# A conditioned transformer block on one core: attention values in the SwiGLU's two PSUM banks, and new instruction orders on four engines

## The reference

```
g, b = t @ gw.T + gb, t @ bw.T + bb                       # per sequence
rmsnorm(x) = g * x * rsqrt(mean(x*x) + 1e-6) + b
x1  = x + attention(rmsnorm_1(x))                         # 16 heads of 16, softmax(q k^T / 4) v, Wo
y   = x1 + (silu(xn @ gate.T) * (xn @ hid.T)) @ out.T     # xn = rmsnorm_2(x1), hidden size 1024
out = x + y
```

## Time and profile before

| what | value |
|---|---|
| median of 3 runs | 1031.92 us (1028.68 to 1034.21) |
| the profiled execution's own time | 1032.31 us |
| its span in the profile | 1030.2 us |
| PE busy | 962.1 us, 93% of the span |
| DVE, ACT, POOL busy | 68%, 54%, 44% |
| one iteration of the loop (start of `scores(t, 0)` to the next) | 60.3 us |
| first `scores(1, 0)` starts at | 87.95 us |
| last iteration with attention (t = 15) starts at | 934.5 us |

### The profile page before, as it was taken

One profiled execution on the slowest core, in us unless ns is written; L12 is line 12 of the kernel. 1 busy time (PEld: TensorE's weight loads), 2 busy tenths in 40 slices (PEclk: granted clock), 3 DMA queues, 4 the chain that ended last, 5 costly groups with the idle time before them and its releaser, 6 DMA issues.

```text
span 1030.2 us, 24455 instructions
## 1 busy us (share of the span) xinstructions
PE 962.1 (93%) x9136; PEld 818.9 (79%) x9136; DVE 699.1 (68%) x1178; ACT 559.6 (54%) x1271; POOL 452.9 (44%) x393
## 2 busy tenths in 40 slices
PE   5667999999999999999999999999999999999898
PEld 4556887878888787888878788887878788788777
DVE  3465767676776768677676867767687776768652
ACT  4444655555565555646555554655656565565442
POOL 3523534454453445435244543534355353435342
PEclk9888999999999999999999999999999999999999
DMA  4100001010100101000010100001010000100000
GB/s 157 62 2 21 1 3 42 1 41 0 32 9 0 41 0 41 0 24 17 0 41 0 41 0 20 20 0 41 0 41 0 20 20 0 41 0 21 1 21 21
DMA packets 18971, 21.71 MB, mean 21 GB/s; under 512 B 640, under 2 KB 18240, under 8 KB 18816
## 3 DMA queue, kind: packets, MB, share of 16 engines
q1 hardware_dynamic: 18720, 21.24, 6.2%
q10 hardware_dynamic: 224, 0.10, 0.1%
HBM read 12.95 MB, written 8.39 MB: 21 GB/s over the span
## 4 chain that ended last, share of the span: by engine, by line
PE 61%; DVE 15%; ACT 11%; issue 9%; POOL 1%; ACTq 1%; DMA 0%; DVEq 0%; SPq 0%; POOLq 0%
PE ps L830 6%; PE ps L832 5%; PE ps L831 5%; PE ps L942 5%; PE ps L958 5%; PE ps L961 4%; PE ps L959 4%; PE ps L950 4%; PE ps L943 4%; PE ps L907 4%; PE ps L915 4%; PE ps L931 3%; DVE row_max L628 3%; DVE sums L642 3%; ACT xn L361 3%
## 5 line engine op out<-in xcount | busy, mean ns | idle before, releaser
L251 POOL TENSOR_TENSOR h_lo<-h,h_hi 128x512 fp32r<-128x512 f32 x128 | 167.6, 1309 | 98.9 <-ACT h_hi L411 92.0
L257 POOL TENSOR_TENSOR probs<-probs,recip 128x512 f32<-128x512 f32 x128 | 134.1, 1054 | 77.7 <-DVE recip L647 75.5
L830 PE MATMUL ps<-out_w_hi,h_hi 128*128 128x256 f32 x512 | 150.6, 294 | 1.1
L832 PE MATMUL ps<-out_w_hi,h_lo 128*128 128x256 f32 x512 | 145.0, 283 | 0.0
L831 PE MATMUL ps<-out_w_lo,h_hi 128*128 128x256 f32 x512 | 144.8, 283 | 0.0
L406 ACT ACTIVATE shared<-ps 128x512 f32<-128x512 f32 x128 | 76.6, 598 | 110.5 <-PE ps L950 109.2
L670 DVE SCALAR_TENSOR_TENSOR shared<-shared,ps 128x512 f32<-128x512 f32 x128 | 87.2, 681 | 72.5 <-ACT shared L406 72.5
L416 ACT ACTIVATE probs<-probs 128x512 f32<-128x512 f32 x128 | 79.3, 638 | 97.5 <-DVE probs L635 97.5
L411 ACT CAST h_hi<-h 128x512 fp32r<-128x512 f32 x128 | 79.1, 618 | 78.6 <-DVE h L677 76.8
L942 PE MATMUL ps<-xn_hi,gate_w_hi 128*128 128x512 f32 x256 | 109.2, 427 | 11.1 <-DVE shared L670 11.0
L830 PEld LDWEIGHTS ps<-out_w_hi,h_hi 128*128 128x128 f32 x512 | 97.2, 190 | 12.1 <-POOL h_lo L251 9.7
(11 more groups left out here) (92 smaller groups left out, 2234.8 us busy)
## 6 DMA issues: line engine op xcount, KB each, us to landing
x_in<-in_x SPq DMA_DIRECT2D x16, 512.0 KB, 3.4
out<-result SPq DMA_DIRECT2D x15, 512.0 KB, 3.0
shared<-in_attT SPq DMA_DIRECT2D x1, 1024.0 KB, 6.4
shared<-in_gateT SPq DMA_DIRECT2D x1, 1024.0 KB, 8.4
shared<-in_hidT SPq DMA_DIRECT2D x1, 1024.0 KB, 4.7
shared<-in_outT SPq DMA_DIRECT2D x1, 1024.0 KB, 5.6
out<-result SPq DMA_DIRECT2D x2, 256.0 KB, 2.2
result<-in_modT SPq DMA_DIRECT2D x1, 256.0 KB, 4.4
```

The lines of the kernel that those rows point to most:

```text
L251: nc.gpsimd.tensor_tensor(h_lo[:, j % KEPT, :], h[:, j % 2, :], h_hi[:, j % KEPT, :].bitcast(F32), ALU.subtract).then_inc(h_lo_done, 1)
L257: nc.gpsimd.tensor_tensor(own, own, recip[:, p % TOGETHER, :].unsqueeze(2).to_broadcast([P, SEQS, L]), ALU.mult).then_inc(divided, 1)
L830: nc.tensor.matmul(dst, a_hi, b_hi, start=first, stop=False, skip_group_check=skip)
L832: return nc.tensor.matmul(dst, a_lo, b_hi, start=False, stop=last, skip_group_check=skip)
```

## The change

It consists of four things.

- The first round's `values_probs(t, 0)` writes GATE and HIDDEN in place of PAIR and PAIR+1 (`attention_bank`). `scores(t, 1)` loses its wait for `attT_done` and follows directly. The wait stands now ahead of `transpose_norm1(t + 1)`, which writes GATE and HIDDEN. In front of `values_probs(t, 0)`, `down(u, 2)` waits ahead of its last block for the sixth h and for the four transposed pairs (before, `gate(u, 5)` held that wait).
- The steady order of PE moves `gate(u, 2)`, `hid(u, 2)` ahead of `down(u, 0)`, puts `down` 1 and 2 ahead of round 2 and 3 and 4 behind `transpose_norm1`, puts `project_q(0)` ahead of `project_k(0)`, `project_k(1)` ahead of `gate(u, 7)` and `project_v(1)` ahead of `down(u, 5)`. DVE, ACT and POOL have new lists too. DVE now does `results(t-2)` ahead of `low_norm2`, `row_maxima(t, 1)` after `hidden(0)`, `scale_rows` ahead of `second_heads(t, 0)`, and `second_values` ahead of `scale_second_rest`. ACT has `keep_input` behind `tanh(3)`, and in the second half `exp(4)`, `second_norm1`, `high_norm1(0)`, `tanh(6)`, `high_norm1(1)`, with `high_attention(0)` after them. POOL has `low_hidden` 4 and 5 straight behind `inverse_rms(t+1)`, then `divide(4)` and the two `low_norm1`; `low_hidden(7)` comes before `low_norm2`.
- Iterations 0 and 15 have lists of their own on all four engines (`first_tile`, `last_tile`). On ACT the first one begins with `keep_input`, `high_weights(2)`, `mean_squares(1)`, `exp(0)`, `exp(1)`, and holds `high_weights(3)` between `keep_transposed` 2 and 3; on POOL `low_weights(3)` stands behind `divide(7)`. On PE iteration 15 runs all of the first three `down` before `scores(t, 1)`.
- At the start POOL waits for `scaled1`, that is for `scale_rows` of tile 0, before it forms the attention weights' low parts.

No arithmetic is added or removed, except that `first_tile` has 22 clock-keeping products (`keep_clock_up`) where there were 24.

```diff
+        def attention_bank(r):
+
+            return (GATE, PAIR + 2)[r]
+
         def heads_of(r, head):
 
-            return ps[:, PAIR + 2 * r:PAIR + 2 * r + 2, :].rearrange(
+            first = attention_bank(r)
+            return ps[:, first:first + 2, :].rearrange(
                 "p s (k h q) -> p (s k) h q", h=2, q=L)[:, :, head, :]
 
...
+            pool.wait_ge(scaled1, 1)
             for part in range(2):
...
-                if mlp:
-                    low_hidden(t - 1, 2)
+                if mlp:
+                    low_hidden(t - 1, 3)
                 if ahead:
                     inverse_rms(t + 1, ms1, ms1_done, mse1, mse1_done, inv1, inv1_done, scaled1)
                 if mlp:
-                    low_hidden(t - 1, 3)
+                    low_hidden(t - 1, 4)
+                    low_hidden(t - 1, 5)
+                if attend:
+                    divide(t, 4)
                 if ahead:
                     low_norm1(t + 1, 0)
-                if attend:
-                    divide(t, 4)
-                if mlp:
-                    low_hidden(t - 1, 4)
-                if ahead:
                     low_norm1(t + 1, 1)
                 if attend:
...
                 if attend:
                     first_heads(t, 0)
                     exp(t, 4)
-                    high_attention(t, 0)
-                if mlp:
-                    high_hidden(t - 1, 5)
-                if ahead:
+                if ahead:
+                    second_norm1(t + 1, GATE + 1)
                     high_norm1(t + 1, 0)
-                    second_norm1(t + 1, GATE + 1)
                 if mlp:
...
-                else:
-                    pe.wait_ge(attT_done, ROUNDS * t + r)
...
-                            last = nc.tensor.matmul(ps[g * ROWS:(g + 1) * ROWS, PAIR + 2 * r + seq, tok],
+                            last = nc.tensor.matmul(ps[g * ROWS:(g + 1) * ROWS, attention_bank(r) + seq, tok],
...
+                    if probs_of is not None and k == BLK - 1:
+                        pe.wait_ge(h_done, CHUNKS * u + 6)
+                        wait_for_probs(probs_of, 0)
...
+            def first_tile(t, attend, mlp, finish, ahead):
+                u = t - 1
+                pe.wait_ge(mod_done, 4 * CH)
+                scores(t, 0)
+                keep_clock_up(12)
+                transpose_probs(t, 0)
+                keep_clock_up(3)
+                transpose_probs(t, 1)
+                keep_clock_up(3)
+                transpose_probs(t, 2)
+                keep_clock_up(3)
+                transpose_probs(t, 3)
+                keep_clock_up(1)
+                wait_for_probs(t, 0)
+                values_probs(t, 0)
+                scores(t, 1)
+                pe.wait_ge(attT_done, ROUNDS * t + 1)
+                for c in range(CH):
+                    transpose_norm1(t + 1, c, GATE + c)
+                project_q(t + 1, 0)
+                transpose_probs(t, 4)
+                transpose_probs(t, 5)
+                project_k(t + 1, 0)
+                transpose_probs(t, 6)
+                transpose_probs(t, 7)
+                project_v(t + 1, 0, probs_of=t)
+                values_probs(t, 1)
+                project_k(t + 1, 1)
+                project_out(t)
+                project_q(t + 1, 1)
+                project_v(t + 1, 1)
+                for c in range(CH):
+                    transpose_norm2(t, c)
...
                     hid(u, 0)
                     gate(u, 1)
                     hid(u, 1)
+                    gate(u, 2)
+                    hid(u, 2)
                     down(u, 0)
-                    gate(u, 2)
-                if filled:
-                    keep_clock_up(FILL_STEP)
+                    gate(u, 3)
                 if attend:
                     transpose_probs(t, 0)
                 if mlp:
-                    hid(u, 2)
-                    gate(u, 3)
                     hid(u, 3)
-                if filled:
-                    keep_clock_up(FILL_STEP)
+                    gate(u, 4)
+                    hid(u, 4)
                 if attend:
                     transpose_probs(t, 1)
                 if mlp:
-                    gate(u, 4)
-                if filled:
-                    keep_clock_up(FILL_STEP)
+                    down(u, 1)
+                    gate(u, 5)
                 if attend:
                     transpose_probs(t, 2)
                 if mlp:
-                    hid(u, 4)
-                if filled:
-                    keep_clock_up(FILL_STEP)
+                    hid(u, 5)
                 if attend:
                     transpose_probs(t, 3)
-                if filled:
-                    keep_clock_up(FILL_STEP)
-                if mlp:
-                    gate(u, 5, probs_of=t if attend else None)
+                if mlp:
+                    down(u, 2, probs_of=t if attend else None)
                 elif attend:
                     wait_for_probs(t, 0)
                 if attend:
                     values_probs(t, 0)
-                if mlp:
-                    hid(u, 5)
-                if filled:
-                    keep_clock_up(FILL_STEP)
-                if attend:
                     scores(t, 1)
                 if ahead:
-                    if mlp:
-                        pe.wait_ge(h_done, CHUNKS * u + 6)
+                    pe.wait_ge(attT_done, ROUNDS * t + 1)
                     for c in range(CH):
                         transpose_norm1(t + 1, c, GATE + c)
                 if mlp:
-                    down(u, 1)
-                    down(u, 2)
+                    down(u, 3)
+                    down(u, 4)
                     if ahead:
                         pe.wait_ge(gained1, t + 2)
+                    elif attend:
+                        pe.wait_ge(attT_done, ROUNDS * t + 1)
                     gate(u, 6)
-                    down(u, 3)
-                if attend:
-                    transpose_probs(t, 4)
-                if mlp:
                     if ahead:
                         pe.wait_ge(xn1_second, t + 2)
                     hid(u, 6)
-                    down(u, 4)
-                if ahead:
+                if attend:
+                    transpose_probs(t, 4)
+                if ahead:
+                    project_q(t + 1, 0)
                     project_k(t + 1, 0)
-                    project_q(t + 1, 0)
                 if attend:
                     transpose_probs(t, 5)
+                if ahead:
+                    project_q(t + 1, 1)
+                if attend:
                     transpose_probs(t, 6)
-                if ahead:
-                    project_q(t + 1, 1)
-                if attend:
                     transpose_probs(t, 7)
                 if ahead:
                     project_v(t + 1, 0, probs_of=t)
...
                     wait_for_probs(t, 1)
                 if attend:
                     values_probs(t, 1)
+                if ahead:
+                    project_k(t + 1, 1)
                 if mlp:
                     if ahead:
                         pe.wait_ge(q_act_done, t + 2)
                     gate(u, 7)
-                if ahead:
-                    project_k(t + 1, 1)
                 if attend:
                     project_out(t)
                 if mlp:
                     if ahead:
                         pe.wait_ge(q_dve_done, t + 2)
                     hid(u, 7)
+                if ahead:
+                    project_v(t + 1, 1)
+                if mlp:
                     down(u, 5)
-                if ahead:
-                    project_v(t + 1, 1)
                 if attend:
                     for c in range(CH):
                         transpose_norm2(t, c)

```

More of the change, by code:

```diff
@@ L481, in iteration @@
[L481 to L482 removed]
+                    tanh(t - 1, 4)
                 if attend:
@@ L732, in first_residual, with first_tile @@
                                             x_res[:, 2 * half:2 * half + 2, :], ALU.add).then_inc(x1_done, 1)
-            def iteration(t, attend, mlp, finish, ahead):
+            def first_tile(t, attend, mlp, finish, ahead):
+                row_maxima(t, 0)
+                row_maxima(t, 1)
+                shift(t, 0)
+                shift(t, 1)
+                reciprocals(t, 0)
+                row_maxima(t, 2)
+                reciprocals(t, 1)
+                row_maxima(t, 3)
+                shift(t, 2)
+                shift(t, 3)
+                reciprocals(t, 2)
+                reciprocals(t, 3)
+                scale_rows(t + 1, x_in, inv1, inv1_done, x_scaled1, xT1_done, scaled1)
+                second_heads(t, 0)
+                low_attention(t, 0)
+                row_maxima(t, 4)
+                first_norm1(t + 1, GATE)
+                row_maxima(t, 5)
+                shift(t, 4)
+                row_maxima(t, 6)
+                shift(t, 5)
+                reciprocals(t, 4)
+                reciprocals(t, 5)
+                shift(t, 6)
+                row_maxima(t, 7)
```

(61 more changed lines are left out.)

339 lines of the change are left out of this document (250 added, 89 removed).

## The result

The changed kernel takes 1025.42 us (median of 8 runs, 1024.73 to 1027.53); beside it the kernel before took 1031.26 (8 runs). The ratio is 0.9948, 95% interval 0.9928 to 0.9969: about 0.5% faster, where 1.5% was forecast. The forecast was 1016. The interval leaves out 1, so a change of 0.5% could be told from none here, which the prediction had thought impossible.

What follows compares the result with a forecast made beforehand. The prediction took the loop as bound by PE and the start by chains through other engines. 1032.3 - 10.3 (start) - 7.0 (loop) + 1.7 (end) = 1016.7, less 0.4: 1016 us, range 1006 to 1026.

Steps and rivals of the forecast that it cites:

- Start, -10.3: Everything up to the start of iteration 1: 10.3 us shorter, bounds -4.2 and -12.
- The 4.2 us of the shared lock: Tile 0's scale_rows, unblocked by GpSimd, takes 1.1 us, so PE's first transposes begin 4.2 us earlier.
- Loop, "I take -0.5 us an iteration": Iterations 1 to 14: 0.5 us less each, -7 us together, bounds +4 and -17.
- the walk: New lists followed through one loop iteration with measured durations; it closed at 59.8 us against 60.3.
- The prediction's own list of idle times: PE's idle pieces in a loop iteration, summed: 3.4 us before, 3.2 after, less what restarts cost.
- End, +1.7, bounds 0 and +3: Iterations 15 and 16 together: 1.7 us longer, from +2.2 and -0.5.
- The +2.2 for `values_probs(1)`: Iteration 15: second-round values products come 2.2 us later, their cover having been spent.
- The -0.5 for iteration 16: Iteration 16: 0.5 us shorter, since gate and hid have fewer stalls.
- the start gains, the loop doesn't: Rival: projections 1.5 us late instead of 1.0, through tanh(6) in their chain; 1023 us, chance 0.17.
- The load of tile t+1: Rival in the loop: later load delays mean_squares and PE beyond 0.6 us of slack; 1037 us, slower chance 0.04.
- the two signs named for being wrong: In the profile after: projections' wait above 1.5 us, or mean_squares waiting for its load.
- the period: Sign in the loop: one iteration takes 59.8 us, against 60.3 before.

Runs made afterwards that it cites:

- e1: Kernel before, with only GpSimd's wait for tile 0's scaled rows added ahead of the attention weights' low parts: 1028.9 us, ratio 0.998.
- e6: Changed kernel with 12 clock-keeping products into unused bank PAIR between down(5) and the second norm's transposes of iteration 15: 1024.9 us.
- e2: Changed kernel with low_hidden(5) moved on GpSimd to just ahead of low_hidden(6): 1019.8 us, ratio 0.9884.
- e3: Changed kernel with tanh(6) moved on ScalarE behind the second high_norm1: 1020.1 us, ratio 0.9886.
- e7: Changed kernel with iteration 15 as in the kernel before on all four engines, first-round values products in PAIR and PAIR+1: 1023.9 us, ratio 0.9925.
- e5: Changed kernel with low_norm2 ahead of results on VectorE in iteration 16 alone: 1026.3 us.
- e8: Changed kernel with the four mends of e2, e3, e5 and e7 together: 1016.2 us, ratio 0.9847.
- e9: Changed kernel with 11 clock-keeping products behind the second norm's transposes of iteration 0: 1023.4 us, ratio 0.9919.
- e11: e4 with 8 clock-keeping products into the GATE bank between the first round's values products and scores(t,1): 1060.9 us, ratio 1.028.
- e4: Changed kernel with first-round values products back in PAIR and PAIR+1, scores(t,1) waiting for attT_done, iteration 15 in loop order: 1084.8 us, ratio 1.052.
- e10: e8 with the 11 clock-keeping products of e9: 1012.8 us, ratio 0.9816.

## Why the prediction was off

- **Start, -10.3: nearly right.** Measured -8.5, and -8.9 to -10.0 in the six other executions with these lists. The 4.2 us of the shared lock are shown by e1 (4.0 at the transposes). In the fastest of the six (e6) the values products came at 43.2 (43.3 walked), the first projection at 53.0 (53.2), iteration 1 at 77.9 (77.7).
- **Loop, "I take -0.5 us an iteration": the term that failed.** It measured -0.08, so that what was forecast as 7 us was 1 us in the loop, and iteration 1 lost 0.4. The waits in it stand where the walk put them: `gate(1)` and `gate(2)` late for `silu` (seen in the rows, removed in no run), the transposes late through the lock (e2 gave 0.39 back), the projections through the chain with `tanh(6)` (idle 0.79; e3 gave 0.46 back). The size failed. It was the difference of two numbers near 60, one measured (60.3) and one walked (59.8), and the walk was 0.4 short: 0.15 up to the projections, and the rest behind them, where no single wait of that size stands in the trace, so its place stays open. The prediction's own list of idle times gave 3.4 before and 3.2 after, a gain of 0.2, and I took the larger figure. And that list compared unlike things: before had 0.4 of small ones, after had none; with them the two are 3.4 and 3.6, no gain at all. The traces say the same: in iteration 7 PE is idle for 60.30 - 58.55 = 1.75 us before and for 60.22 - 58.42 = 1.80 after. The 0.81 at `gate(1)` and the 0.20 at `project_q(1)` went, 0.32 at the transposes and 0.79 at the projections came.
- **End, +1.7, bounds 0 and +3: mis-sized.** The +2.2 for `values_probs(1)` is exact (973.02 to 985.16 against 966.13 to 978.29 is the same distance, and the values products came 40.68 us into the iteration, 38.48 before); with the old lists (e7) the second transposes come 1.9 us earlier. Missing was a price for the idle time that the cover's loss left behind `down(5)`: from the second transposes to the first gate of iteration 16 it takes 6.43 us, 5.28 before, and 4.75 with the clock kept (e6). Behind it came the wait for `low_norm2` in that gate, with `results` ahead of it: 0.9 us in e5 at a low clock, 0.2 between e7 and e8 at a clock of 1.00. The -0.5 for iteration 16 was eaten by them. How much of this an execution shows differs; the whole end lost 3.1 to 4.4 us with the same lists.
- **Iteration 1.** It was 2.2 us longer than the loop's already in the kernel before (62.5), and I carried it as an ordinary iteration. e9 shows the cause, the low clock after the idle time ahead of its first scores.
- **Rivals.** The one whose number came is "the start gains, the loop doesn't" (1023). Its stated cause did not come, so the number is luck: it wanted the projections 1.5 us late, and they were 1.0 late as walked. The load of tile t+1 never held up ScalarE in the loop. Neither of the two signs named for being wrong came (a wait of the projections above 1.5 us, `mean_squares` waiting for its load); the sign that did was the period, 60.2 and not 59.8, with every row of the loop near its place.

## What to carry to other kernels

When a loop is 97% busy on one engine, an order's worth is a small difference of waits: sum the waits on both sides, item by item, and don't subtract a walk from a measured period, since a walk can be short by the few tenths that are at stake (0.4 us here). A wait in such a loop has two sides, the engine's own work and the chain it waits for: shortening one gives only as much as the other allows, so two mends that gave 0.4 and 0.5 gave 0.5 together. Price a long idle piece of TensorE twice, once for itself and once for the slow products behind it, and try products into a free bank in it (e6, e9 and e11 each gained by them). Here slow products followed the pieces of 2.65 and 3.44 us in every execution and those of 2.0 to 2.2 us in some. And take a stage's gain from more than one profile where the clock moves in it: one profile put the end's loss at 4.4 us, two others with the same lists at 3.1 and 3.3.

## What the runs showed of the hardware

- With a gap of 2.2 us once in an iteration (other idle pieces 0.8 and 0.6 us) the granted clock fell in nine of 13 iterations and stayed at 1.00 in four: scores of 2.01 us or 3.6 to 3.7, iterations of 62.1, 63.7 and 65.3 us (e4). With the gap filled all were equal (e11). A gap of 2.0 us ahead of the second transposes of iteration 15 was followed by a low clock in the kernel before and in e10, and by none in e7 and e8, and the list there is the same in e8 and e10. How long the clock stays low is not constant either: the first 10 us of iteration 1 were granted 0.66 in the changed kernel's profile and 0.54 in that of e8, with the same lists there. What decides between them is open.
- VectorE's `scale_rows`, SBUF to SBUF, gets its instructions in one at a time between GpSimd's passes: four take 1.14 us with GpSimd idle (e1), 2.06 beside one pass (e2), 3.07 beside two and 5.31 beside two long ones. The Trainium skill, "SBUF — State Buffer", section "Terms", says that the port pair is held for a full instruction and the loser blocks; these four numbers agree, and they show besides that each GpSimd pass costs VectorE one wait and not the whole group. Not every instruction that reads SBUF is held up: the sums over a 128x512 tile in SBUF take 0.63 to 0.69 us beside a GpSimd pass and without one.
